# Maxima one slot later in the attention loop, and the negation in a batch's second step

## What is computed

```python
q = jnp.einsum('bse,hed->bhsd', x, Wq) + bq[None, :, None, :]     # 16 heads of 16
k = jnp.repeat(kg, per, axis=1)                                   # 4 groups of K and V
scores = jnp.einsum('bhqd,bhkd->bhqk', q, k) * (1.0 / np.sqrt(d))
scores = jnp.where(causal[None, None, :, :], -jnp.inf, scores)
attn = jax.nn.softmax(scores, axis=-1)
out = jnp.einsum('bhqk,bhkd->bhqd', attn, v)
...
x = x + 0.5 * _L0_ffn_ref(_layernorm(x, axis=-1), ...)
x = x + _L0_attn_ref(_layernorm(x, axis=-1), ...)
x = x + 0.5 * _L0_ffn_ref(_layernorm(x, axis=-1), ...)
```

## Time and profile before

| | us |
|---|---|
| runs of before | 388.37 median of 3 (387.34 to 390.03) |
| profiled execution | 389.66 |
| its span, first to last instruction | 387.9 |
| PE busy in the span | 353.7 (91%) |
| DVE busy | 230.5 (59%) |
| ACT busy | 145.5 (38%) |
| POOL busy | 170.9 (44%) |

### The profile page before, as it was taken

One profiled execution on the slowest core, in us unless ns is written; L12 is line 12 of the kernel. 1 busy time (PEld: TensorE's weight loads), 2 busy tenths in 40 slices (PEclk: granted clock), 3 DMA queues, 4 the chain that ended last, 5 costly groups with the idle time before them and its releaser, 6 DMA issues.

```text
span 387.9 us, 8428 instructions
## 1 busy us (share of the span) xinstructions
PE 353.7 (91%) x3162; PEld 285.7 (74%) x3168; DVE 230.5 (59%) x707; ACT 145.5 (38%) x308; POOL 170.9 (44%) x281
## 2 busy tenths in 40 slices
PE   7599999999999787999999999789899999999980
PEld 3359999999967455667676676466699999999660
DVE  4988945222332688787887878589568974223220
ACT  3222111111111244577875877477641111111110
POOL 2040432466112226267878757375703335662220
PEclk9779999999999999999999999899999999999995
DMA  8969950249701547413615335000300102498000
GB/s 268 410 208 363 345 197 29 68 168 335 299 25 49 196 109 101 106 35 72 111 32 121 77 55 112 24 28 30 101 24 29 55 29 66 139 344 331 27 26 13
DMA packets 28003, 50.01 MB, mean 129 GB/s; under 512 B 4812, under 2 KB 21584, under 8 KB 26930
## 3 DMA queue, kind: packets, MB, share of 16 engines
q1 hardware_dynamic: 20082, 24.89, 22.6%
q0 software_dynamic: 4656, 21.83, 15.9%
q10 hardware_dynamic: 3216, 2.67, 2.5%
HBM read 34.88 MB, written 6.82 MB: 107 GB/s over the span
## 4 chain that ended last, share of the span: by engine, by line
PE 70%; DVE 10%; DMA 7%; SPq 5%; issue 3%; POOL 2%; ACT 1%; POOLq 0%; DVEq 0%
PE bank L1138 30%; PE bank L1164 14%; PE bank L1613 3%; PE bank L1563 3%; PE bank L1645 3%; SPq L1507 3%; DMA area<-JV 2%; SPq L1524 2%; DVE mxa L1580 2%; PE bank L1098 2%; PE bank L1126 2%; PE bank L903 2%; PE bank L1390 2%; DMA area<-x2d 1%; DMA area<-x 1%
## 5 line engine op out<-in xcount | busy, mean ns | idle before, releaser
L1138 PEld LDWEIGHTS bank<-area,W 128*128 128x128 f32 x1024 | 119.0, 192 | 2.3 <-ACT area L1242 0.8
L1138 PE MATMUL bank<-area,W 128*128 128x128 f32 x1024 | 120.0, 275 | 0.2 <-ACT area L1242 0.2
L1323 DVE TENSOR_TENSOR area<-area,bank 128x512 f32<-128x512 f32 x34 | 23.4, 687 | 65.4 <-issue 43.3
L1164 PE MATMUL bank<-W,area 128*128 128x256 f32 x256 | 60.9, 381 | 0.0
L1623 ACT ACTIVATE area<-bank 128x512 f32<-128x512 f32 x96 | 54.6, 596 | 15.3 <-PE bank L1613 13.6
L1580 DVE TENSOR_REDUCE mxa<-bank 128x2 f32<-128x512 f32 (+2 forms) x96 | 51.4, 552 | 10.6 <-PE bank L1567 10.3
L1253 ACT ACTIVATE area<-bank 128x512 f32<-128x512 f32 x34 | 20.3, 597 | 97.5 <-PE bank L1138 91.1
L1632 POOL TENSOR_SCALAR_AFFINE_SELECT area<-area 128x512 f32<-128x512 f32 x64 | 41.0, 649 | 35.9 <-ACT area L1623 35.5
L1164 PEld LDWEIGHTS bank<-W,area 128*128 128x128 f32 x256 | 46.1, 190 | 5.8 <-issue 0.8
L980 POOL DMA_INDIRECT out<-area,sidx x17 | 17.0, 1002 | 57.8 <-DVE area L1308 55.6
L980 POOL DMA_INDIRECT x2d<-area,sidx x17 | 17.7, 1042 | 56.2 <-DVE area L1308 44.6
(11 more groups left out here) (217 smaller groups left out, 511.0 us busy)
## 6 DMA issues: line engine op xcount, KB each, us to landing
W<-wall SPq DMA_DIRECT2D x24, 512.0 KB, 6.7
area<-area SPq DMA_DIRECT2D x42, 128.0 KB, 3.7
area<-x SPq DMA_DIRECT2D x8, 256.0 KB, 5.9
area<-x2d SPq DMA_DIRECT2D x8, 256.0 KB, 5.6
rows<-area ACTq DMA_DIRECT2D x8, 256.0 KB, 2.7
area<-JV SPq DMA_DIRECT2D x40, 32.0 KB, 3.2
area<-area SPq DMA_DIRECT2D x12, 64.0 KB, 2.7
area<-x,gidx POOLq DMA_INDIRECT x18, 3.7
```

What stands on the lines that cost most here:

```text
L1138: last = pe.matmul(ps[:, i * P:(i + 1) * P], W[:, w:w + P], xT[:, j % 2, c, :], start=(c == 0), stop=(c == C - 1))
L1164: last = pe.matmul(y, hT[:, n % 2, i, :], W[:, bass.ds(off + at, H)] if mixed(n) else W[:, off + at:off + at + H], start=(i == 0), stop=(i ...
L1323: v.tensor_tensor(out, sil[:, n % 2, :], bank[2 + n % 2][:], ALU.mult).then_inc(f_h[l], 1)
```

## The change

`AHEAD` (7 head groups) becomes `LEAD` (20 units): slot u of step n now holds unit 3n+20+u, not 3n+21+u, and 20 units run ahead of the loop, not 21. The negation of batch b+1 moves in DVE's program from the end of step 4b to step 4b+1, behind the maximum of slot 0.

```diff
-AHEAD = NG + 3
+LEAD = 3 * (NG + 3) - 1
...
-    at = 3 * (n + AHEAD) + u
+    at = 3 * n + LEAD + u
...
-            for n in range(3 * AHEAD):
+            for n in range(LEAD):
                 a_max_pe(n)
...
-            for n in range(3 * AHEAD):
+            for n in range(LEAD):
                 a_max_dve(n)
...
                 for c in chunks(n, 0):
                     a_max_dve(c)
+                if g == 1 and b + 1 < B:
+                    a_neg_dve(b + 1)
                 if pair:
                     a_heads_sum(n // 2 - 1, seen)
...
                 for c in chunks(n, 2):
                     a_max_dve(c)
-                if g == 0 and b + 1 < B:
-                    a_neg_dve(b + 1)
```

## The result

| | before | after |
|---|---|---|
| median of six runs each, us | 388.69 (387.32 to 390.03) | 392.73 (390.03 to 395.16) |
| profiled execution, us | 389.66 | 395.16 |
| its span | 387.9 | 393.4 |
| its mean granted clock | 0.972 | 0.967 |
| PE idle in the loop, stretches over 0.12 us | 6.6 | 10.4 |

The changed kernel is slower: 1.0115 of before, 95% interval 1.0075 to 1.0154, 4.0 us between the medians. A second measurement beside other runs of before gave 393.25 against 389.13, and 1.0169 (1.0119 to 1.0219). The ratios leave disturbed runs out on both sides, so they need not be the quotient of the medians. The forecast was 390.7 with a range up to 392.2: right in direction and place, short in size, 4.0 us of loss where 2.35 was forecast.

What follows compares the result with a forecast made beforehand. PE's waits in the attention loop were taken to bound the kernel. Terms -0.52 - 0.45 - 0.22 + 2.22 + 0.52 + 0.4 + 0.4 = +2.35 us, carried to the median 388.37, gave 390.7, range 387.6 to 392.2.

Steps and rivals of the forecast that it cites:

- Landings: PE's waits for stacked queries and keys: step 9's goes (-0.52), step 21's falls from 2.65 to 2.20 (-0.45).
- Entrance: At the loop's entrance a scores pair fills most of PE's 0.32 us wait before unit 20: -0.22.
- The negation: On DVE in steps 1, 5, 9, 13, 17: held by GpSimd's mask, 0.5 to 0.65 us; PE's transposes wait 0.4 or more.
- DVE's chain: DVE's work up to slot 0 of step 4b+3 grows by 0.74 with a long negation, 0.29 with a short one.
- step 3: Slot 0 there waits for DVE's longer chain: +0.74, one of three such steps making +2.22.
- step 7: Slot 0 there waits for DVE's longer chain: +0.74, the transpose's wait included.
- steps 11, 9: Step 9's landing wait goes (-0.52), but DVE loses that gain to the negation, so step 11 adds +0.52.
- step 15: PE's 0.48 wait for the row of negated maxima hides part of DVE's lateness: +0.4.
- Rival (d): Slower: lateness puts other DVE work against masks, three places by 0.3 more, and step 25 pays 1.1: 392.3; chance 0.12.
- Step 25: PE's transpose comes 1.1 late behind the last negation, step 26's 0.81 wait goes; 0.4 let through.
- The clock: Behind step 21's wait before ran 3.40 us at half clock, costing 1.4; the shorter wait might or might not keep it.
- rival (b): The clock stays up in step 22, the rest as forecast: 390.7 - 1.4 = 389.3; chance 0.12.

Runs made afterwards that it cites:

- e2: The kernel before with the negation written as a reduction (a maximum over one element, negated) in its old place; 388.7 us against 389.1, ratio 1.0020.
- e3: The kernel before, units 21 ahead, with only the negation moved to step 4b+1 behind slot 0; 390.7 us against 388.5, ratio 1.0095.
- e3b: The kernel before, with only the negation moved behind V's addition in step 4b+1; 392.3 us against 389.1, ratio 1.0113.
- e1: The changed kernel with the negation written as a reduction over one element, in the same place; 390.7 us against 388.5 for before, ratio 1.0038.
- e8_delay: The changed kernel with the negation as a reduction and an extra maximum (about 0.45 us) ahead of it in steps 1, 5, 9, 13, 17; 393.4 us, ratio 1.0150.
- e4: The changed kernel with GpSimd normalising a tile ahead of its mask in steps 4b+1 of batches 0 to 3; 390.7 us against 388.5, ratio 1.0102.

## Why the prediction fell short, step by step

**Landings.** Step 9's wait went, as forecast, but in e2, e3 and e3b it went too, with units 21 ahead. So the forecast was right in outcome, which may be luck: the runs don't show that the later slot did it. Step 21 waits 1.60 (1.13 in the second profile), where 2.20 was forecast. The shift of a slot is worth 0.51 (2.57 in e2, 2.06 in e1), close to the 0.45 of the forecast. The rest is PE arriving later: slot 0 of step 19 now waits 0.93 in place of e1's 0.20, behind the release of that stack, and so eats into the landing's wait. In the forecast the two stood side by side; they overlap.

**Entrance.** The wait ahead of unit 20 went, 0.32 for a forecast of 0.22. Unit 18's of 0.37 stayed.

**The negation.** As forecast in every part: five long ones, 0.62 to 0.63, each started 0.04 to 0.05 into a mask, the transposes waiting 0.47 to 0.53. By the Trainium skill (SBUF — State Buffer, section "Who interferes with whom") a multiplication by a constant out of and into SBUF can take the pair of ports that GpSimd works through, a reduction never does, an operation on two tensors takes it when both lie in SBUF, and whichever side starts first holds it. The traces agree: 0.63 against 0.18 for the two forms of the negation in the same place, 0.28 for V's addition (one input in PSUM) whether or not a mask runs, 0.84 for line 1491 and 0.65 for line 1698 (both inputs in SBUF), and in e3b the mask that waits (0.78). They do not show that it is held to the very end: that mask grew by 0.15, while line 1491 ran on for 0.29 behind the mask's start.

**DVE's chain: the step that failed.** The sum held the chain's growth at 0.74 a batch, with everything behind the negation at its old duration. In steps 5, 9, 13 and 17 it came to 1.40 to 1.47, since that very growth put lines 1491 and 1698 behind masks (e8_delay shows it without a long negation). The table sets PE's time from one batch's projections (line 1390) to the next against the forecast's terms.

| from step to step | before | after | difference | forecast |
|---|---|---|---|---|
| 0 to 4 | 14.44 | 15.10 | +0.66 | +0.74 (step 3) |
| 4 to 8 | 15.34 | 16.82 | +1.48 | +0.74 (step 7) |
| 8 to 12 | 16.75 | 16.88 | +0.13 | +0.52 - 0.52 (steps 11, 9) |
| 12 to 16 | 15.81 | 16.89 | +1.08 | +0.40 (step 15) |

The sum of these is 3.35 where the forecast had 1.88, and the excess lies in the second and the fourth line, 0.74 and 0.68. The first line agrees by luck: line 1491 takes 0.43 more there too, but line 1698 of step 2 was held in before and isn't in after. DVE in step 2 of before, then of after:

```profile
171.80 0.90 DVE L1698 TENSOR_TENSOR area<-area,at 128x256 f32<-128x256 f32 x1
```

```profile
173.80 0.43 DVE L1698 TENSOR_TENSOR area<-area,at 128x256 f32<-128x256 f32 x1
```

The rows for the second and third line of the table are PE's, of before

```profile
178.74 0.38 PE L1390 MATMUL bank<-area,wq_s 128*128 128x256 f32 x1
...
194.08 0.38 PE L1390 MATMUL bank<-area,wq_s 128*128 128x256 f32 x1
...
210.83 0.38 PE L1390 MATMUL bank<-area,wq_s 128*128 128x256 f32 x1
```

and of after

```profile
180.33 0.43 PE L1390 MATMUL bank<-area,wq_s 128*128 128x256 f32 x1
...
197.15 0.43 PE L1390 MATMUL bank<-area,wq_s 128*128 128x256 f32 x1
...
214.03 0.43 PE L1390 MATMUL bank<-area,wq_s 128*128 128x256 f32 x1
```

Before had one slow batch, 16.75 us long, and three quicker ones; after has three of that length. The slow one could have been read beforehand: DVE was late in step 9 of before, by the landing, and its timeline there shows what lateness does:

```profile
199.95 0.85 DVE L1491 TENSOR_TENSOR kr<-kv,JV 64x256 f32<-64x256 f32 x1
...
203.37 0.70 DVE L1698 TENSOR_TENSOR area<-area,at 128x256 f32<-128x256 f32 x1
```

The prediction explained that batch's wait of 0.74 by DVE being held, and took over 0.52 of it; it did not ask which of DVE's instructions had grown. Rival (d) named the mechanism, at 0.3 in three places. It came to 0.66 to 0.73 in four (steps 5, 9, 13 and 17), of which before had already paid the second.

**Step 25.** The transpose waits 1.58 (1.1 + 0.37 forecast), the heads' wait in step 26 fell from 0.81 to 0.20: 0.6 net, where 0.4 was forecast.

**The clock.** The forecast kept the fall behind step 21. It did not come: rival (b)'s condition, worth the 1.4 it named, so that from step 16's projections to the end of the loop after is 0.2 quicker, not 0.69 slower, though one unit more stands there (and one fewer ahead of step 0, where after is 0.69 quicker). It hides part of the loss: from the first scores of the loop to the router's matmuls behind it (line 674) after takes 118.8 us (160.2 to 279.0) and before 116.4 (158.6 to 274.9); with before's fall of about 1.4 taken off, the difference is 3.9, close to the 3.8 of the idle time. That the 2.4 of the two profiles comes near the forecast's sum of 2.35 is luck.

**Numbers.** 0.48 stood on the forecast and 0.12 on rival (d), whose 392.3 was nearest to the 392.7 measured. The range ended at half of (d). The fault was less the width than that a delay, taken for certain, was not followed along DVE's program to the next masks.

## What to carry to other kernels

When an edit makes an engine later by half a microsecond, go on along its program. Take each instruction that shares something with another engine, and ask whether it still starts first; a batch of the old trace that was late for some other reason shows what happens. Where a small operation must run beside GpSimd's work, its form decides: here a reduction over one element in place of a multiplication took 0.18 us for 0.63 in the same place. And don't add up waits that stand one behind another on the path: a new wait behind a release shortens the wait for what was released.

## What was not expected of the hardware

- A few hundredths of a microsecond decide who waits: a negation 0.01 ahead of a mask took 0.17 us, one 0.04 behind 0.63. The mask pays as well when it is second: 0.77 to 0.86 in place of 0.63.
- The clock in the loop did not follow the length of the wait alone. Behind step 21's waits of 2.65, 2.64, 2.60, 2.55, 2.06 and 2.02 us the granted clock was half for a while; behind 1.72, 1.60, 1.23, 1.13, 0.93 and 0.41 it stayed at full. Behind step 25's wait of 1.58 it fell in e1 and e8 and stayed in both profiles of after; behind e4's 1.86 there, and behind the 2.57 of step 21 in e2, it stayed too:

```profile
245.50:249.00 3.50, 3.43 (x45) 2.67 (x46) 2.95 (x10) 2.06 (x4) 0.83 (x2) 1.00 0.00 0
```

- Runs of one and the same kernel spread over 2% with the granted clock (before: 384.5 to 392.6 us, with clocks of 0.983 to 0.962), more than any of the effects studied here. Most of the waits named here came out within some hundredths of a microsecond in two traces of one kernel, where five rounds of timing left half a per cent open.
